# Cross-attention's preparation, second norm and rounding, one step per slot, through the PSUM bank of PV

## What is computed

```python
x = layernorm(x + self_attention(x))          # 16 heads of 128, q, k and output normed, ALiBi, causal
kv_c, q_c = ctx @ W_kvc, x @ W_dq             # 64 and 96 wide
scores = (q_nope . k_nope + rope(q_rope) . rope(k_rope)) * scale, masked to a band of 9 keys
x = layernorm(x + (softmax(scores) . v) @ W_o)
gate, up = sigmoid(q(x) @ q(w_gate)), q(x) @ q(w_up)
x = layernorm(x + q(gate * up) @ q(w_down))   # q: activations to 8 bits per token, weights to -1, 0, 1
```

## Time and profile before

| | us |
|---|---|
| median of 3 runs (1564.73 to 1569.97) | 1565.81 |
| profiled execution, its own time | 1570.61 |
| its span, first to last instruction | 1568.8 |
| PE busy, share of the span | 92% |
| ACT, DVE, POOL busy | 81%, 79%, 76% |
| mean granted PE clock | 0.970 |

### The profile page before, as it was taken

The page is one execution under the profiler, slowest core; times in us unless marked ns, Lnnn a source line. Parts: engine busy times, 40 slices in busy tenths (PEclk is TensorE's granted clock), DMA queues, the critical chain, the costliest instruction groups (busy, mean ns, idle before and its releaser), DMA issues. The chain is left out here.

```text
span 1568.8 us, 54176 instructions
## 1 busy us (share of the span) xinstructions
PE 1441.5 (92%) x20146; PEld 1059.8 (68%) x20146; DVE 1234.5 (79%) x2876; ACT 1264.4 (81%) x4006; POOL 1195.8 (76%) x1131
## 2 busy tenths in 40 slices
PE   5998999999999999999999996878999999946997
PEld 3666777777777777777777774435777777733665
DVE  3877777777777777777777787878898988847997
ACT  4877888888888888888888884658889999956776
POOL 4899889888989989888988884546777777710655
PEclk9999999999999999999999997999999999975999
DMA  6600000000000000000000000204433333310011
GB/s 229 182 10 16 16 3 16 16 3 17 16 3 16 16 3 16 16 3 17 16 3 16 3 2 2 82 20 145 122 109 107 100 110 108 104 29 1 15 41 54
DMA packets 57731, 70.62 MB, mean 45 GB/s; under 512 B 14433, under 2 KB 42401, under 8 KB 57473
## 3 DMA queue, kind: packets, MB, share of 16 engines
q1 hardware_dynamic: 57472, 67.17, 14.2%
HBM read 29.39 MB, written 4.19 MB: 21 GB/s over the span
## 5 line engine op out<-in xcount | busy, mean ns | idle before, releaser
L420 DVE SCALAR_TENSOR_TENSOR X<-projP,r,X 128x256 f32<-128x256 f32 x512 | 211.2, 475 | 3.3 <-PE projP L254 3.2
L234 PEld LDWEIGHTS svP<-W,xT 128*128 128x128 bf16 x3072 | 182.3, 98 | 30.2 <-DVE scores L407 0.2
L205 PE MATMUL qkssP<-xT,W 128*128 128x512 bf16 x768 | 189.6, 383 | 13.9 <-POOL W L485 11.4
L480 POOL TENSOR_TENSOR y_sql<-y_sq 128x512 bf16<-128x512 f32 x128 | 133.3, 1041 | 80.4 <-ACT y_sq L321 80.1
L234 PE MATMUL svP<-W,xT 128*128 128x128 bf16 x3072 | 192.4, 219 | 0.0
L205 PE MATMUL kP<-xT,W 128*128 128x512 bf16 x768 | 186.8, 379 | 0.0
L254 PE MATMUL projP<-W,y 128*128 128x256 bf16 x1024 | 178.0, 276 | 3.3 <-POOL yl L480 3.2
L1073 POOL TENSOR_TENSOR qhl<-qh 128x1024 bf16<-128x1024 f32 x64 | 121.3, 1895 | 74.0 <-issue 63.5
L971 ACT ACTIVATE x_probs<-xsP,x_ntop 128x64 f32<-128x64 f32 x512 | 153.0, 329 | 28.6 <-DVE x_ntop L1021 27.4
L336 ACT ACTIVATE probs<-scores,ntop 128x64 f32<-128x64 f32 x512 | 170.4, 339 | 1.7 <-DVE ntop L410 1.7
L480 POOL TENSOR_TENSOR k_sql<-k_sq 128x512 bf16<-128x512 f32 x128 | 133.3, 1041 | 21.4 <-ACT k_sq L341 20.8
(11 more groups left out here) (200 smaller groups left out, 4749.2 us busy)
## 6 DMA issues: line engine op xcount, KB each, us to landing
x_turned<-x_turn SPq DMA_DIRECT2D x128, 128.0 KB, 2.1
oB<-oA SPq DMA_DIRECT2D x256, 64.0 KB, 2.1
w_stage<-in_wqkvp SPq DMA_DIRECT2D x16, 512.0 KB, 3.3
x_stage<-in_xT SPq DMA_DIRECT2D x8, 512.0 KB, 4.2
X<-in_x SPq DMA_DIRECT2D x1, 4096.0 KB, 17.3
x_stage<-in_ctxT SPq DMA_DIRECT2D x8, 512.0 KB, 3.6
out<-X SPq DMA_DIRECT2D x7, 512.0 KB, 2.9
okv<-in_L_xattn_W_o SPq DMA_DIRECT2D x1, 2048.0 KB, 11.7
```

Of the source, the lines that this page charges most:

```text
L205: last = nc.tensor.matmul(dst[:, :], weight(parity, u, i, c), xT[:, z, c, tok], start=(c == 0 and k == 0), stop=(c == CC - 1 and k == 2))
L234: last = nc.tensor.matmul(svP[:, b * D:(b + 1) * D], xT[:, u, c, t * TILE + b * P:t * TILE + (b + 1) * P], weight(parity, z, 2, c), start= ...
L420: last = nc.vector.scalar_tensor_tensor(acc, projP[:, b * C:(b + 1) * C], r[:, PB + b:PB + b + 1], acc, ALU.mult, ALU.add)
L480: return nc.gpsimd.tensor_tensor(dst[:, :], src[:, :], high(src, slice(None), 0, TILE), ALU.subtract)
```

## The change

The block `prepare_cross` is replaced by a short one, `start_cross`, that prepares tile 0 alone and does the folds, and norms tile 1 on ACT. What it did for the other tiles is cut into eight steps a tile, one a slot: in slot n = 8j+g PE does step g for tile j+1, in the bank `oP` that PV also uses, and ACT copies it out (`copy_out`) before PV may write again. Steps 0 and 1 of a slot are the transposes of the rounded X of tile j-3, so the FFN preparation lies in the slots as well, with 18 slots instead of 7 after slot 63 (`LAST`). PE's order in a slot is now scores, PV, rope and latent, the step, transposes, projection. PV comes one slot later. Buffers of all tiles become two of one tile, and high parts are read in place from float32 (every second bf16) in rope, latent, scores and products. The keys' transposed product becomes four transposes. Low parts of weights and of context tile 0 are made on DVE in self-attention's slots 20 to 24; the rest by POOL.

```diff
+        ffn = ffn_buffers(sb)
...
+            cross_attention(nc, a, X, norm1, ident, late, ffn, sem, lambda n, s, d: sb(n, s, d, part), part)
...
+            feed_forward(nc, X, ident, ffn, out, sem, lambda n, s, d: sb(n, s, d, part), part)
...
+            def low_weights(k):
+                qr, qrl, stage = late["qr"], late["qrl"], late["x_stage"]
+                half = H * R // 2
+                if k == 0:
+                    dve.wait_ge(late["s_weights"], late["weights"])
+                    for c in range(CC):
+                        low_of(nc.vector, late["dql"][:, c, :], late["dqf"][:, c, :])
+                        low_of(nc.vector, late["kvl"][:, c, :], late["kvf"][:, c, :])
+                elif k < 3:
+                    dve.wait_ge(s_qkw, 2)
+                    cols = slice((k - 1) * half, k * half)
+                    low_of(nc.vector, qrl[:, cols], qr[:, cols])
+                else:
+                    dve.wait_ge(late["s_ctx"][0], 16)
+                    low_of(nc.vector, late["low_ctx"][:, k - 3, :], stage[:, 0, k - 3, :])
             def slot(g, j, n, has):
...
+                    if LOW_AT <= j < LOW_AT + 3 + CC:
+                        low_weights(j - LOW_AT)
...
+            pe.wait_ge(late["s_weights"], late["weights"])
+            kv_product(nc, kvP, late, 0).then_inc(s_kv, 1)
+            fold(0)
+            fold(1)
+            pe.wait_ge(s_kf, 1)
+            nc.tensor.matmul(krP[:, :], wkr[:, :], kf[0:KVC, 0, :], start=True, stop=True).then_inc(s_kr, 1)
+            for b in range(PB):
+                last = nc.tensor.transpose(tkP[:, b * KVC:(b + 1) * KVC], kf[0:KVC, 0, b * P:(b + 1) * P], ident[0:KVC, 0:KVC])
+            last.then_inc(s_tk, 1)
+            fold(2)
+            pe.wait_ge(s_norm, 1)
+            for c in range(CC):
+                for b in range(PB):
+                    last = nc.tensor.transpose(xtP[c][:, b * P:(b + 1) * P], X[:, b, c * P:(c + 1) * P], ident[:, :])
+                last.then_inc(s_xt, 1)
+            fold(3)
+            pe.wait_ge(s_xl, CC)
+            qc_product(nc, qcP, late, xf, xl).then_inc(s_qc, 1)
+            fold(4)
+            fold(5)
...
+            act.wait_ge(norm.s_shift, 1)
+            for b in range(PB, 2 * PB):
+                norm.by_scalar(b)
...
+            pool.wait_ge(s_KV, 1)
+            low_of(nc.gpsimd, KVl[:, 0], KVf[:, 0].rearrange("p b n -> p (b n)"))
+            for c in range(CC):
+                pool.wait_ge(s_xf, c + 1)
+                low_of(nc.gpsimd, xl[:, c, :], xf[:, c, :]).then_inc(s_xl, 1)
+            pool.wait_ge(s_kadd, 1)
+            low_of(nc.gpsimd, kl[:, 0, :], kf[:, 0, :])
+            pool.wait_ge(s_qcf, 1)
+            low_of(nc.gpsimd, qcl[:, 0, :], qcf[:, 0, :])
+            pool.wait_ge(s_flo, len(folds))
...
+def low_of(eng, dst, src):
+    return eng.tensor_tensor(dst, src, high_part(src), ALU.subtract)
...
-    S_AT, T_AT, PV_AT, PROJ_AT = 3, 4, 5, 7
+    S_AT, T_AT, PV_AT, PROJ_AT = 3, 4, 6, 7
+    LAST = N + 2 * HP + 2
+    WEIGHTS_AT = N
...
+        j, g = divmod(n, HP)
+        kind, c, tile = (("xq", 0, j - 3), ("xq", 1, j - 3), ("xt", 0, j + 1), ("kv", 0, j + 1),
+                         ("xt", 1, j + 1), ("kr", 0, j + 1), ("qc", 0, j + 1), ("tk", 0, j + 1))[g]
+        return (kind, c, tile) if 0 <= tile < NT and (kind != "xq" or n < LAST) else (None, 0, 0)
...
+            load_ctx(2)
+            for n in range(LAST):
+                j, g = divmod(n, HP)
+                if has(n, PV_AT):
...
+                if step(n)[0] == "kr":
+                    wait(sp, s_kturn, turns_before(n + 1))
+                    wait(sp, s_kadd, turns_before(n))
+                    sp.dma_start(moved_k[0:R, :], turned_k[R:P, :]).then_inc(s_kmoved, 16)
+                if g == 4 and j + 3 < NT:
+                    wait(sp, s_step, steps_before(n))
+                    load_ctx(j + 3)
+                if 1 <= n < 4:
+                    ffn_weights(n - 1, ("wgT", "wuT", "wdT")[n - 1])
...
+            def other(n):
+                kind, c, tile = step(n)
+                if kind is None:
+                    return
+                wait(pe, s_oe, min(max(n - PV_AT + 1, 0), N))
+                wait(pe, s_out, outs_before(n))
+                wait(pe, s_kturn, turns_before(n))
+                if kind == "xq":
+                    wait(pe, s_xs, tile + 1)
+                    for b in range(PB):
+                        last = nc.tensor.transpose(oP[:, b * P:(b + 1) * P], xs[:, b, c * P:(c + 1) * P], ident[:, :])
+                elif kind == "xt":
+                    wait(pe, s_ln1, tile - 1)
+                    for b in range(PB):
+                        last = nc.tensor.transpose(oP[:, b * P:(b + 1) * P], X[:, tile * PB + b, c * P:(c + 1) * P], ident[:, :])
+                elif kind == "kv":
+                    wait(pe, s_low_ctx, CC * tile)
+                    last = kv_product(nc, oP, late, tile)
...
+                elif kind == "qc":
+                    wait(pe, s_xl, CC * tile)
+                    last = qc_product(nc, oP, late, xf, xl)
...
                 if has(n, PV_AT):
                     m = n - PV_AT
+                    tile = m // HP
                     wait(pe, s_ptl, m + 1)
                     wait(pe, s_oe, m)
+                    wait(pe, s_out, outs_before(n))
+                    wait(pe, s_kturn, turns_before(n))
+                    wait(pe, s_KVl, tile)
...
+                if has(n, 0):
+                    tile, g = divmod(n, HP)
+                    wait(pe, s_qcl, tile)
+                    qc = high_part(qcf[:, tile % 2, :]), qcl[:, tile % 2, :]
+                    rope_w = high_part(qr[:, g * P:(g + 1) * P]), qrl[:, g * P:(g + 1) * P]
+                    wait(pe, s_qh, n - 1)
...
+                other(n)
...
+                if n == WEIGHTS_AT + 3:
+                    wait(pe, late["s_abs"], 3)
+                    wait(pe, s_lat, N)
+                    nc.tensor.matmul(latP[:, 0:3], kept["ones"][:, :], late["w_sums"][:, :], start=True, stop=True).then_inc(s_sum, 1)
...
+            def copy_out(n):
+                kind, c, tile = step(n)
+                if kind in (None, "kr"):
+                    return
...
+                if kind == "xq":
+                    last = nc.scalar.activation(xqT[:, c, tile * TILE:(tile + 1) * TILE], oP[:, :], ACT.Copy, bias=-MAGIC)
+                elif kind == "xt":
+                    last = nc.scalar.activation(xf[:, c, :], oP[:, :], ACT.Copy)
+                elif kind == "kv":
...
+                last.then_inc(s_out, 1)
...
+            LN1_BLOCKS = {1: (0,), 3: (1,), 5: (2, 3)}
+            for n in range(LAST):
+                j, g = divmod(n, HP)
+                if has(n, PV_AT):
+                    m = n - PV_AT
+                    wait(act, s_o, m + 1)
+                    wait(act, s_ot[m % 2], 64 * (m // 2))
+                    nc.scalar.activation(oA[:, m % 2].rearrange("p i (b t) -> p b i t", b=PB), oP[:, :].rearrange("p (b i t) -> p b i t", b=PB, i=2),
+                                         ACT.Copy).then_inc(s_oe, 1)
                 if has(n, S_AT):
...
+                copy_out(n)
...
+                if j + 2 < NT and g in LN1_BLOCKS:
+                    for b in LN1_BLOCKS[g]:
+                        last = norm.by_scalar((j + 2) * PB + b)
+                    if g == 5:
+                        last.then_inc(s_ln1, 1)
+                u = j - 2
+                if g == 2 and 0 <= u < NT:
+                    own = slice(u * PB, (u + 1) * PB)
+                    wait(act, s_mom, NB // NT * (u + 1))
+                    nc.scalar.activation(rstd2[:, own], moments[:, own, 1], ACT.Ln, bias=norm.eps_col[:, :]).then_inc(s_ln, 1)
+                    wait(act, s_ln, u + 1)
+                    nc.scalar.activation(rstd2[:, own], rstd2[:, own], ACT.Exp, scale=-0.5).then_inc(s_root, 1)
+                k = n - WEIGHTS_AT
+                cols = CC * DFF
                 if 0 <= k < 3:
...
+                if 4 <= k < 7:
+                    w = late["okv"][:, (k - 4) * cols:(k - 3) * cols]
+                    wait(act, s_winv, 1)
+                    nc.scalar.activation(w, w, ACT.Identity, bias=ffn["magic"][:, :], scale=winv[:, k - 4:k - 3]).then_inc(s_wm, 1)
+            nc.scalar.preload_act_table_set("sigmoid_and_others")
...
+                if g == 7 and 1 <= j <= NT:
+                    acc = X[:, (j - 1) * PB:j * PB, :]
+                    wait(dve, s_proj, HP * j)
+                    nc.vector.tensor_tensor(acc, projP[:, :].rearrange("p (b c) -> p b c", b=PB), acc, ALU.add).then_inc(s_acc, 1)
...
+                kind, _, tile = step(n)
+                if kind == "kr":
+                    wait(dve, s_step, steps_before(n + 1))
+                    wait(dve, s_kmoved, 16 * (tile - 1))
+                    nc.vector.tensor_tensor(by_token(turned_k[:, :]), by_token(oP[:, :]), tabs[:, 2, :].unsqueeze(1).to_broadcast([P, BT, T]),
...
```

(122 more changed lines are left out.)

481 lines of the change are left out of this document (158 added, 323 removed).

## The result

Over four runs of each on one chip the changed kernel took 1554.39 us and the kernel before 1566.53: the ratio is 0.9925 (95% interval 0.9908 to 0.9942), 12 us faster. I had forecast 32.

A forecast was written before the change was run, and what follows sets the result against it. Chains of waiting engines surround cross-attention slots where PE and ACT are full, so the change trades chain time for slot time: 3 - 51 + 43 + 1 - 28 = -32, put onto the median of 1565.81: 1534 us, range 1514 to 1561.

The forecast's parts named there:

- Part 3: The 63 slots of cross-attention: +43 us, from 41 of added PE work and 2 more of stalls.
- the layout of POOL: POOL's operations laid out in a slot: it just keeps up in most, with stalls of 3 us a tile.
- Rival A: Slots cost more than PE's work, through POOL and DVE collisions or strided columns: 1553 us; with rival D 0.25.
- My 1556 by that rule: In the slots, each DVE norm block could wait for a whole `qhl` of 1.9 us: sum about -10, 1556 us.
- Rival B: In the slots, the steps fill the present stalls, which fall to 3 us: 1517 us; chance 0.13.
- Rival C: In the slots, a late swap transfer holds up DVE: slower than before, 1590 us at 6.5 a slot; chance 0.12.
- Rival D: FFN's first matmul still waits for weights or X, saving 10 instead of 28: 1552 us; with rival A 0.25.
- the signs of being wrong: In the slots: DVE waiting for `x_turned` in most, PV waiting for `copy_out`, or slots above 6 us.
- Part 4: The ramp-down after the slots: +1 us, bounds 0 to 4, for the weights' rounding on ACT.
- Part 5: The FFN preparation after the last projection: -28 us, 14.7 against 42.8, bounds 24 to 30 saved.
- Part 2: The preparation block after self-attention: -51 us, 72.5 down to about 21, bounds 45 to 54 saved.
- Part 1: Self-attention: +3 us, for low parts on DVE in five slots, between 0 and 8.

The follow-up runs named there:

- e1: The changed kernel with POOL's extra operations (low parts, rounding of X) ahead of `qhl` instead of behind it: 1535.02 us, ratio 0.9808.
- e7: e1 with the third weight's absolute sum, the roundings and DVE's rounding of that weight moved later: 1536.06 us, ratio 0.9817.
- e3: The changed kernel with PE's and ACT's earlier order, PV still six slots late, transfers in the slot of their `oA`: 1607.68 us, ratio 1.0246.
- e5: The changed kernel with PE's and ACT's earlier order, PV five slots late and transfers one slot behind PV, as before the change: 1551.87 us, ratio 0.9919.
- e9: e1 with POOL's extras spread over slots and kf's sum on POOL, plus the three edits of e5: 1530.99 us, ratio 0.9772.
- e11: e1 with POOL's extras spread over slots, kf's sum on POOL, and PV's extra lag undone from slot 66 on: 1528.8 us, ratio 0.9739.
- e4: The changed kernel with ACT's absolute sums and first rounding of the FFN weights over 16 columns instead of 1024: 1550.36 us, ratio 0.9892.

## Why the prediction was wrong

The direction and the side of most terms were right, the size was not: 12 us instead of 32. Part of it is the base: I put a difference of spans onto the median, as if the 4.8 us by which the profiled execution of before was longer would stay in both kernels. They did not, so the 17 us by which the spans differ are 12 on the medians. The rest by its steps:

**Part 3, the slots, +54 instead of +43: this failed.** PE's work was as summed. Rope's three matmuls stayed at their length with every second bf16 as operand: 1215.26 - 1214.59 = 0.67 us in e1, against 1360.51 - 1359.86 = 0.65 before, so that term, kept at 0, was right. What failed was the layout of POOL, "POOL just keeps up in most slots" and 3 us of stalls a tile; they were nearly 5. I added POOL's operations in the order in which they stand and saw the projection's wait, but took a wait of 0.4 for `qcl` where it was about 0.8, let a tile's last slot and the next cost 1.4 together where they cost 2.9 (7.2 + 5.9 us, of which PE's work is 10.2), gave slot 2 no stall where it had 0.8, and never asked what POOL did before `qhl`. Slot 4, for which I had 1.5 by DVE's norm, had about 1. POOL's idle time was in the forecast's own rows, 51.5 us of it: I read it as room, and the order made it unusable. e1 shows it: with the same work in front of `qhl` the slots take 347.5 us instead of 365.9. That e1's 1535 us is also the number forecast is in part luck: its slots are 7 us shorter than I had them, which makes up for a ramp-down 5 us longer and for the base.

**Rival A** (1553) had the time and half of the mechanism: POOL's chain decides, in the main as an order, and not through a longer norm or the columns. Its time was luck: it gave the slots 19 us more than the forecast, where they took 11, and the ramp-down and the base made up the rest; and with six norms before slot 63, not seven, its own sum would be 16. DVE's norm took 3.10 us in each full tile, against my 2.8 and the rival's 4.16. The collision is real, though: beside the norm it struck kf's sum, 1.93 us where I had 0.7. The Trainium skill (SBUF — State Buffer, Who interferes with whom) has this as an exclusive lock between GpSimd and a DVE operation with two SBUF inputs or in a two-port mode. The rows of kf's sum, which has two SBUF inputs, agree. In e7 POOL's rounding took 3.69 us instead of 1.89 beside DVE operations of one input; by that rule they would be in a two-port mode, which no trace shows. My 1556 by that rule in the prediction has no working behind its -10.

**Rival B** did not come: the stalls grew, and of the steps only the transposes of the rounded X were hidden, in waits that the change itself had made. **Rival C** did not either, DVE waited 1.9 us for the swap; e3 shows that the path is there and costs 53 us once `oA` comes late. **Rival D** did not come: the wait ahead of the FFN shrank by 25.7 us, not 10. Of the signs of being wrong only slots above 6 us were seen, in half of a tile's slots; the mean was 5.8.

**Part 4, the ramp-down, +6 instead of +1, beyond its bound of 4.** I had written that the last transfer must wait for the projection two before it anyhow. What I left out is that with a lag of six PV of the last pairs stands behind a projection that waits for a transfer, so that the chain runs through both. e5, e9 and e11 put it at 5.6 to 6 us. ACT's sum counts together with it (3.9 us in e4), and next to nothing without the extra lag (e5, e9).

**Part 5, -26 instead of -28,** within the bounds. DVE rounds the third weight, 2.5 us, between the last sum into X and its statistics, which my list of small operations lacked.

**Part 2** was right: 23.0 us of block against 21 forecast. **Part 1** cannot be judged: self-attention's 3 us cannot be told from its drift.

## What to carry to other kernels

When an engine works on several things by a hand-written order, ask of each operation who waits for it and how soon, and put the one with a slot's slack last: an idle stretch in front of it is usable only by what stands ahead. A lag that costs nothing in the steady slots is paid at the end of the pipeline, and can be undone there alone. And before moving work "beside" a chain, look which engine the chain is on: work on a neighbour can lengthen it, as DVE's rounding did POOL's by 1.8 us in e7.

## What was unexpected of the hardware

DVE's sum of two SBUF tiles took 1.93 to 2.39 us beside POOL's 1.89 us operation, where its twin with a PSUM operand took 0.69 and the same sum with POOL's operation just over took 0.68: it is held until the neighbour's operation ends. POOL can be held up as well: four roundings took 3.69 us beside DVE's two scalings of 2048 columns, which have one input each, and 1.83 to 1.89 in e1 (2.15 to 2.28 in the changed kernel's full tiles, where they start while kf's sum still runs), while DVE's took 1.20 and 1.39 against 1.22 and 1.23 in the changed kernel. So there the one that was held up was POOL, which had started in the midst of DVE's.
